# A decoder layer on one core: no unread matmuls in TensorE's first waits, first layer norm rebuilt turned by GpSimd from group 4 on, all static orders set anew

## The reference, cut to what matters

```
x = x + linear_attention(layernorm(x))     # q,k = elu(.)+1, causal, 16 heads of 16, biases, then Wo
x = x + cross_attention(layernorm(x), ctx) # softmax over 128 keys, 16 heads of 16
x = x + ffn(layernorm(x))                  # silu(w1)*w2, gelu(h1), gelu(h2), w3; 256 -> 1024 -> 1024 -> 1024 -> 256
layernorm(x) = (x - mean) / sqrt(var + 1e-5)
```

## Time and profile before

| | us |
|---|---|
| three runs, median (range) | 1068.17 (1066.75 to 1068.72) |
| the profiled execution, its own time | 1067.3 |
| its span, first to last instruction | 1065.5 |
| TensorE (PE) busy | 1041.3 (98%) |
| VectorE (DVE) busy | 769.4 (72%) |
| ScalarE (ACT) busy | 527.6 (50%) |
| GpSimd (POOL) busy | 262.1 (25%) |
| granted TensorE clock, mean | 1.000 |

### The profile page before, as it was taken

One profiled execution on the slowest core, in us unless ns is written; L12 is line 12 of the kernel. 1 busy time (PEld: TensorE's weight loads), 2 busy tenths in 40 slices (PEclk: granted clock), 3 DMA queues, 4 the chain that ended last, 5 costly groups with the idle time before them and its releaser, 6 DMA issues.

```text
span 1065.5 us, 25693 instructions
## 1 busy us (share of the span) xinstructions
PE 1041.3 (98%) x10186; PEld 866.9 (81%) x10186; DVE 769.4 (72%) x1708; ACT 527.6 (50%) x855; POOL 262.1 (25%) x363
## 2 busy tenths in 40 slices
PE   7999999999999999999999999999999999999998
PEld 7989877878877888778788878787888888787886
DVE  5999998767996879867798778987678455523412
ACT  4344553855536635556454556374633635433432
POOL 3323352100441114301161111620026001500600
PEclk9999999999999999999999999999999999999999
DMA  4687766443643444534645334453364435544552
GB/s 161 230 296 244 260 225 209 159 133 105 214 149 125 139 154 144 165 124 135 192 150 169 118 107 156 157 156 115 129 209 157 144 119 199 172 146 158 180 177 80
DMA packets 76742, 174.87 MB, mean 164 GB/s; under 512 B 10960, under 2 KB 26448, under 8 KB 76624
## 3 DMA queue, kind: packets, MB, share of 16 engines
q1 hardware_dynamic: 73168, 161.70, 45.1%
q10 hardware_dynamic: 3456, 11.54, 3.8%
HBM read 145.38 MB, written 39.35 MB: 173 GB/s over the span
## 4 chain that ended last, share of the span: by engine, by line
PE 84%; DVE 10%; issue 2%; DMA 2%; POOL 0%; ACT 0%; SPq 0%; ACTq 0%; DVEq 0%; POOLq 0%
PE bank L1254 43%; PE bank L1141 8%; PE bank L1239 6%; PE bank L1274 6%; PE bank L1113 5%; PE bank L1082 5%; PE bank L1097 3%; PE bank L1087 2%; DVE hidden_full L1020 2%; PE bank L1058 2%; DVE mx L989 2%; DVE hidden_full L1023 1%; PE bank L1191 1%; PE bank L1134 1%; PE bank L1122 1%
## 5 line engine op out<-in xcount | busy, mean ns | idle before, releaser
L1254 PE MATMUL bank<-hidden_a,weight_ring 128*128 128x512 f32 x1024 | 251.3, 396 | 0.0
L1254 PE MATMUL bank<-hidden_b,weight_ring 128*128 128x512 f32 x1024 | 248.1, 395 | 0.3 <-DVE inexact_flag L1045 0.3
L1254 PEld LDWEIGHTS bank<-hidden_b,weight_ring 128*128 128x128 f32 x1024 | 187.8, 188 | 39.4 <-issue 0.8
L1254 PEld LDWEIGHTS bank<-hidden_a,weight_ring 128*128 128x128 f32 x1024 | 187.2, 188 | 40.0 <-issue 1.4
L857 ACT ACTIVATE hidden_full<-bank,columns_sb 128x512 f32<-128x512 f32 x128 | 88.2, 689 | 221.8 <-PE bank L1254 221.3
L706 POOL TENSOR_TENSOR ve<-mv,eps 128x1 f32<-128x1 f32 (+1 forms) x80 | 21.1, 264 | 474.5 <-DVE mv L872 474.5
L1239 PE MATMUL bank<-hidden_b,weight_ring 128*128 128x512 f32 x512 | 123.0, 394 | 1.4 <-DMA weight_ring<-weights_scratch 1.4
L745 POOL TENSOR_TENSOR hidden_a<-hidden_full,hidden_a 128x512 fp32r<-128x512 f32 x64 | 83.0, 1297 | 167.9 <-ACT hidden_a L852 166.7
L1239 PEld LDWEIGHTS bank<-hidden_b,weight_ring 128*128 128x128 f32 x512 | 94.2, 188 | 21.3 <-DMA weight_ring<-weights_scratch 1.8
L1028 DVE TENSOR_TENSOR hidden_a<-hidden_full,hidden_a 128x512 fp32r<-128x512 f32 x64 | 43.6, 683 | 70.8 <-ACT hidden_a L863 70.6
L989 DVE TENSOR_REDUCE mx<-bank 128x4 f32<-128x512 f32 x128 | 80.3, 678 | 16.6 <-PE bank L1141 16.3
(11 more groups left out here) (135 smaller groups left out, 1696.4 us busy)
## 6 DMA issues: line engine op xcount, KB each, us to landing
weight_ring<-weights_scratch SPq DMA_DIRECT2D x160, 512.0 KB, 3.5
weights_scratch<-in_h ACTq DMA_DIRECT2D x16, 512.0 KB, 5.0
xn3T_scratch<-hidden_b SPq DMA_DIRECT2D x16, 512.0 KB, 4.0
weight_bits<-in_h SPq DMA_DIRECT2D x32, 256.0 KB, 3.6
weight_ring<-weights_scratch SPq DMA_DIRECT2D x32, 256.0 KB, 2.8
values_scratch<-hidden_full SPq DMA_DIRECT2D x14, 512.0 KB, 4.6
xv<-values_scratch SPq DMA_DIRECT2D x14, 512.0 KB, 4.2
x_in<-in_x SPq DMA_DIRECT2D x16, 256.0 KB, 2.8
```

Of the source, the lines that this page charges most:

```text
L1254: mm = eng.matmul(pbank(step, g, n)[:, :], ring[:, slot, kk * P:(kk + 1) * P], src[:, part, kk, :], start=(kk == 0 and part == 0), stop=(k ...
```

## The change

1. `FILL` is empty: the 104 unread matmuls are gone.
2. From group 4 on (`REMADE = 4`) the first layer norm is made on the turned tile. A turned copy of the input, `xT`, comes in as a further input (made on the host from `x`). `load_x` and the statistics stay; then `x_in` is overwritten by the turned `x` (`load_xT`), mean and `rstd` go to HBM (`keep_stats1`) and come back broadcast over all partitions, one after the other, into one buffer (`load_stats1` 0 and 1), and GpSimd subtracts and multiplies in place (`xn1` 0 and 1, two instructions of 128x256 each). ScalarE and VectorE read `x_in` where they read a bank. `ln1` on VectorE and `ln1T` on TensorE are gone for these 12 groups.
3. At the start ScalarE loads its table before it waits for the constants, and makes `s1h` at its first `q`; VectorE takes the first group's statistics before it waits for the columns; the load of the columns stands behind those of `wq` and `wk`.
4. `LEAD`, `OFFSET`, `PATIENCE` (14.5 to 17.2), the assumed start times and `AT` are other numbers, so all five lists come out anew. Weight copies are asked for from 12.9 us on every 10.06 us (before: from 31.4 every 7.60), the pieces of `load_bits` from 280.3 on every 12.22 us (before: from 159.9 every 15.64).

```diff
+    REMADE = 4
-    SPARE, PATIENCE, HOLD, MANY = 1, 14.5, 0, 3
+    SPARE, PATIENCE, HOLD, MANY = 1, 17.2, 0, 3
...
-    LEAD = {("gpsimd", "bias"): 18.2, ("gpsimd", "ctx"): -146.3, ("gpsimd", "gate_rest"): -222.4,
+    LEAD = {("gpsimd", "bias"): 282.9, ("gpsimd", "ctx"): -679.5, ("gpsimd", "gate_rest"): -407.6,
...
-        steady("ln1", vector=-12.6, took=dict(vector=.75))
-        steady("ln1T", tensor=-10.5, scalar=-8.63, vector=-7.75, took=dict(tensor=.4, scalar=.52, vector=.6))
+        if g < REMADE:
+            steady("ln1", vector=-12.6, took=dict(vector=.75))
+            steady("ln1T", tensor=-10.5, scalar=-8.63, vector=-7.75, took=dict(tensor=.4, scalar=.52, vector=.6))
+        else:
+            steady("load_xT", sync=-30, took=dict(sync=5))
+            steady("keep_stats1", sync=-25, took=dict(sync=2.2))
+            for n in range(2):
+                steady("load_stats1", n, sync=-24 + 4 * n, took=dict(sync=3))
+                steady("xn1", n, gpsimd=-20 + 4 * n, took=dict(gpsimd=1.75))
+            steady("ln1T", scalar=-8.63, vector=-7.75, took=dict(scalar=.52, vector=.6))
...
-    AT |= {("scalar", "copy_weights", j): 31.4 + 7.60 * j for j in range(NCH)}
-    AT |= {("sync", "load_bits", i, j): 159.9 + 15.64 * (NWB * i + j) for i in range(8) for j in range(NWB)}
+    AT |= {("scalar", "copy_weights", j): 12.9 + 10.06 * j for j in range(NCH)}
+    AT |= {("sync", "load_bits", i, j): 280.3 + 12.22 * (NWB * i + j) for i in range(8) for j in range(NWB)}
...
-                eng.dma_start(cols[:, :], columns).then_inc(cols_loaded, 16)
                 for n, (dst, src) in enumerate(zip(whole, (wqT, wkT, wvT, xkT, xvT, woT, xqT))):
+                    if n == 2:
+                        eng.dma_start(cols[:, :], columns).then_inc(cols_loaded, 16)
...
+                    elif step == "load_xT":
+                        eng.wait_ge(LN1["mean_var"], GB * g + GB)
+                        eng.dma_start(x_t, xT.rearrange("(c p) t -> p c t", p=P)[:, :, T * g:T * g + T]).then_inc(xT_loaded, 16)
+                    elif step == "keep_stats1":
+                        eng.wait_ge(LN1["rstd"], g + 1)
+                        eng.wait_ge(mean1_copied, g - REMADE + 1)
+                        eng.dma_start(st1_d[g].rearrange("w p b -> p w b"), stats1_out[:, :, :]).then_inc(stats1_stored, 16)
+                    elif step == "load_stats1":
+                        eng.wait_ge(stats1_stored, 16 * (g - REMADE + 1))
+                        if n == 1:
+                            eng.wait_ge(xn1_centred, g - REMADE + 1)
+                        elif g > REMADE:
+                            eng.wait_ge(xn1_made, g - REMADE)
+                        eng.dma_start(stats1[:, :, :].rearrange("p s b -> p (s b)"),
+                                      st1_d[g, n].rearrange("s b -> (s b)").partition_broadcast(P)).then_inc(stats1_loaded, 16)
...
+                    elif step == "xn1":
+                        half = x_t.rearrange("p c (b s) -> p c b s", b=GB)
+                        mean_or_rstd = stats1[:, :, :].rearrange("p s b -> p b s")
+                        if n == 0:
+                            eng.wait_ge(xT_loaded, 16 * (g - REMADE + 1))
+                        eng.wait_ge(stats1_loaded, 32 * (g - REMADE) + 16 + 16 * n)
+                        for c in range(C):
+                            last = eng.tensor_tensor(half[:, c], half[:, c], mean_or_rstd, (ALU.subtract, ALU.mult)[n])
+                        last.then_inc((xn1_centred, xn1_made)[n], 1)
...
-                eng.wait_ge(consts_loaded, 16)
                 eng.preload_act_table(ACT.Exp)
+                eng.wait_ge(consts_loaded, 16)
...
-                FILL = {("ln1T", 0, 0): 24, ("q", 0, 0): 20, ("xv", 0, 0): 40, ("lin_scores", 0, 1): 20}
+                FILL = {}
```

118 lines of the change are left out of this document (72 added, 46 removed).

## The result

The changed kernel takes 1079.97 us (median of 4 runs, 1074.07 to 1083.74), the kernel before, on the same chip, 1067.46 (median of 4, 1065.46 to 1068.72). The ratio is **1.0109, with an interval of 1.0074 to 1.0145: slower by 1.1%**. Foretold were 1060.5 us, 1054.5 to 1066.5, so the forecast missed the sign and its range the value. The profiled execution of the changed kernel took 1078.59 us with a span of 1076.8, which is 11.3 us over the span of before.

What follows compares the result with a forecast made beforehand. The prediction took TensorE's instruction list to bound the kernel. Transposes -4.2, start -1.8, order -1.6 and additions 0 summed to -7.6 us: 1059.7 from the profiled 1067.3, or 1060.5 as a median, range 1054.5 to 1066.5.

Steps and rivals of the forecast that it cites:

- term 2: Start of the program, to group 1's q: dropped filling and earlier statistics save 1.8 us, bounds -5.2 to +2.
- term 4: Added GpSimd instructions, SyncE issues and traffic, less VectorE work: 0 us, hidden by TensorE's other work, bounds -4 to +4.
- Term 1: Twelve ln1T transposes leave TensorE at 0.35 us each: 4.2 us saved, bounds 4.2 to 5.4.
- term 3: TensorE's order: fewer returns to 512-column work and from tiled to whole-array work save 1.6 us, bounds 0 and -2.8.
- about twice that: TensorE's order: each return from tiled to whole-array work costs about twice the 0.1 us of a return to 512-column work.
- 0.7 us of waiting: Start: the first lin_scores waits 0.7 us for VectorE's kz, which gets only little earlier.
- stays near 15 us: Whole run: TensorE's idle time beyond the start stays near 15 us.
- My slower rival: SyncE's queue: load_stats1 1 waits for GpSimd and starves the weight ring; 1072, chance 0.07; weak form 1064.5 to 1067, 0.05.
- TensorE waits less: Whole run: new lists and a freer VectorE remove a third of 15 us of waits; 1056 us, chance 0.13.
- The start gives nothing: Start: half pace and waits eat the 1.8 us gain; 1062.3 us, chance 0.10.
- GpSimd holds VectorE up: GpSimd's 48 more instructions delay VectorE through shared ports, waits grow by 2.6 us; 1063 us, chance 0.08.

Runs made afterwards that it cites:

- short start: Kernel before with the change's new start, first normalisation ahead of the split of wq, unread matmuls 18 instead of 24 and 8 instead of 20: 1064.98 us, ratio 0.9978.
- single load: Changed kernel with mean and 1/deviation in one contiguous store and one load instead of two: 1069.53 us, ratio 1.0012.
- combined: Changed kernel with one contiguous statistics store and one load, unread matmuls only inside its waits, and one list move each on VectorE and SyncE: 1067.89 us, ratio 1.0010.
- trimmed: Combined kernel without 40 unread matmuls ahead of max(6,0), 30 instead of 40 ahead of lin_scores(0,0), 20 instead of 30 ahead of x_scores(1,0): 1065.22 us, ratio 0.9981.
- trimmed with the start: Trimmed kernel with VectorE's first normalisation ahead of the split of wq and 18 instead of 24 unread matmuls ahead of the first turned rows: 1064.57 us, ratio 0.9977.
- Experiment 2: Changed kernel with no group remade (REMADE = 16): 1096.88 us, ratio 1.0286; changed kernel's steps with the old tables and old filling: 1091.92 us, ratio 1.0221.
- experiment 4: Changed kernel with unread matmuls put only where its own trace has TensorE waiting: 1075.21 us, ratio 1.0085.
- the two moves: Changed kernel with group 0's kz ahead of the rest of group 1's rows (VectorE), group 6's context load ahead of four ring loads (SyncE): 1075.66 us, ratio 1.0073.
- experiment 6: Changed kernel with GpSimd's subtraction and product on only 16 of the 128 rows: 1073.95 us, ratio 1.0061.
- one load, old store: Changed kernel with one statistics load instead of two, the store kept at two runs of 8 bytes a partition: 1073.23 us, ratio 1.0056.
- combined, with the two VectorE moves: Combined kernel with group 1's kz ahead of the rest of group 2's rows and the rest of xn3T(0,0) ahead of that of ln1T(4): 1068.32 us, ratio 1.0014.
- trimmed, with the start and the two VectorE moves: Trimmed kernel with the start, plus group 1's kz ahead of group 2's remaining rows and the rest of xn3T(0,0) ahead of ln1T(4)'s: 1064.13 us, ratio 0.9967.

## Why the prediction was wrong

The forecast was 19.5 us too low. Three steps of it failed: the start (term 2), the added transfers (term 4, put at nothing), and the waits of the new lists up to the first gate, for which the sum had no term.

**Term 1 and term 3, the transposes and the order: right in size together.** Together -5.8 us were foretold. The rest of the span, computed as in the table above, was 1035.7, 1037.7 and 1036.0 us in three kernels with the old lists (before, before without filling, short start), and 1033.9, 1031.9, 1031.3, 1029.8 and 1031.4 in five with the new ones (changed, single load, combined, trimmed, trimmed with the start). The means are 1036.5 and 1031.7: -4.8 us. It is coarse by about 2 us each. Experiment 2 parts the terms a little. With the new tables but all transposes the rest is 1038.1, 4.2 above the changed kernel (1033.9); with the old tables and twelve transposes fewer it is 1033.3. So the gain goes with the transposes, as term 1 had it (-4.2), and term 3's -1.6 isn't shown. Its "about twice that" for returns from tiled work stood on no row either.

**Term 2, the start: wrong, its sign too.** Measured in the changed kernel: +1.5 us at the `q` of group 1 instead of -1.8. Three other kernels with the same start and lists and no filling had it at 30.81, 31.45 and 32.64, so the sign holds and the size scatters.
- The normalisation started at 7.11, not 6.0. I counted 2.67 us from the statistics on and overlooked that VectorE's list puts the split of `wq` between, which waits for another engine. I had read the gap, not what stood in it.
- The half pace lasted until about 13 us instead of 15, which was better than foretold, and `q`, `k`, `xk` and `v` were done near 17.0, as before (16.9).
- "0.7 us of waiting" for `kz` were 3.27: it now stood behind the rest of group 1 and beside GpSimd's `ctxs`, which doubled its time. I had seen the stretching in the earlier trace rows and made it a rival in proportion to GpSimd's busy time. It costs not by its sum but by which instruction it hits.
- The clock then fell a second time, behind this wait, and again behind three more (experiment 4). I had priced the lost filling at the start alone.

**Between the start and the first gate: no term at all.** From the `q` of group 1 to the first gate the same real work took 115.2 us instead of 105.4. That is 9.9 us more. In the windows from 30 to 140 us the idle time is up by 6.6 us and the clock loss by 3.4, which together are about all of it. Term 3 priced the new order by its returns alone, and the sum took the waits of the old lists as they were ("stays near 15 us"). A part was got back by filling in them (gate 5.8 us earlier, experiment 4), by the two moves (1.0) and in the run with the single load (2.5). In none of the traced kernels with new lists did this stretch take less than 108.4 us; in those with the old lists and filling it took 105.4 to 106.1. Beyond the two `kz` and the late contexts the cause of these waits is open.

**Term 4, what is added: wrong.** I put it at 0 within 4 us either way. Taking out only what I had costed at nothing, a second load and the form of a store, gave 10 us. I had added up the chain of a group, 15 us against 60 to spare, and that nearly held: ScalarE waited for the remade rows twice, 2.2 us and 6.1 us (until 341.4, behind the same store), and TensorE never. GpSimd's 48 instructions took 771 ns and not 942, 36 us in all. What I left out is that SyncE's queue is in order, and that the new steps block it up to twice in a group, 47.8 + 38.8 us in all. My slower rival named the blocked queue, but asked only for the ring (a margin of 7.4 us, which sufficed). The loads with less margin, mask bits and contexts, stood in the same queue. The small store, my estimate 3.4, landed in 5.7.

**The rivals.** "TensorE waits less": it waits 15.2 us more. "The start gives nothing": in the changed kernel it lost. "GpSimd holds VectorE up": VectorE's busy time is 2.3 us lower although 24 normalisations of 603 ns, 14.5 us, have left it, so about 12 us of stretching and slower forms came in. (Two examples: `xn1T` from `x_in` takes 821 ns instead of 671 from a bank, and the product with `rec` 31.0 us in all before and 33.9 now.) That they cost the time foretold isn't shown; experiment 6 speaks for a small part. "SyncE's queue": right in place, and near in price (12 us), wrong in what starves. It had a chance of 0.07 in full. Its price was that of a late ring, which did not happen; that the loss from other loads came near it is luck.

**The place of gain and loss.** The start of the first `gate` parts each trace in two:

| profiled kernel | `q` of group 1 at | first gate at | from there to the end |
|---|---|---|---|
| before | 29.1 | 134.5 | 931.0 |
| before without filling | 28.3 | 138.5 | 929.8 |
| before, short start | 27.6 | 133.6 | 929.3 |
| changed | 30.7 | 145.9 | 930.9 |
| changed, filling in its waits | 29.3 | 140.1 | 934.1 |
| changed, two moves | 28.3 | 144.9 | 928.7 |
| one load, old store | 30.8 | 146.2 | 924.1 |
| single load | 31.5 | 143.4 | 923.4 |
| combined | 29.1 | 139.6 | 926.4 |
| combined, with the two VectorE moves | 28.0 | 136.4 | 923.7 |
| trimmed | 28.2 | 140.3 | 924.3 |
| trimmed, with the start | 26.3 | 136.3 | 923.5 |
| trimmed, with the start and the two VectorE moves | 27.0 | 136.6 | 928.1 |

Behind the gate five of the seven kernels with one load are some 7 us under before. The combined one is 4.6 under, and 2.4 of its time there is the filling at 331 us; the last one is 2.9 under, which stays unexplained. The old lists scatter there too, from 929.3 to 931.0. So the gain behind the gate is about what terms 1 and 3 promised (-5.8), and in the changed kernel it was gone. It came back with the second load's removal; the store's form shows there by less than 1 us. Ahead of the gate the new lists lost 11.4 us, and filling, moves, start and single load together won back 9.6. Alone, filling moved the gate by 5.8, the moves by 1.0 and the single load by 2.5, each in one trace. The gates of the two kernels that differ only in the store's form lie 2.8 us apart (146.2 and 143.4), which I can't explain by it; the `q` of group 1, which no load of statistics precedes, also lies up to 2.0 us apart in kernels with the same start (30.68 to 32.64).

## What to carry to other kernels

Before a step is costed at nothing because it isn't on the path, list what stands behind its wait in every in-order queue, and compare each of those with its own margin, not only the one that was late before. Filling matmuls belong to one schedule: where the wait has gone they are work, and where a new wait has come their absence can cost a second time through the clock. A forecast for a new order needs a term for its own waits: the waits of the old list do not carry over. Tables tuned for one set of steps cost 2 to 3% here with another, so a change of both can only be judged in parts by small moves in the finished list.

## What the runs showed that I had not expected

- Two stores of 2 KB differ by the form of their rows. In two runs of 8 bytes a partition the statistics landed in 5.0 to 5.9 us (medians in four kernels), in 16 contiguous bytes in 3.7 to 4.2 (six kernels). The older store of 16 bytes took 2.7 to 3.0 in the same six, so 0.9 to 1.4 us of the difference from it isn't the form.
- A transfer behind four ring loads of 512 KB on one queue took 11.4 us from issue to landing, where the median of its kind is 4.5.
- Two VectorE instructions that take 0.87 us together took 1.81 beside one GpSimd instruction of 1.27, and 1.91 beside another.
- An order can lose where no new instruction stands: 9.9 us between the `q` of group 1 and the first gate, with the same real work on TensorE.
- Most kernels with the new lists scatter more: the trimmed one from 1060.6 to 1071.8, the short start from 1062.7 to 1067.1, in 12 runs each. Why is open.
